# Another fill and drain for a group-normed dynamic 3x3 convolution block

## The chip, the cores and the metric

One core of a Trainium2 chip runs the kernel. The metric is the device time of one execution in microseconds (us). The engines are TensorE (PE), VectorE (DVE), ScalarE (ACT), GpSimd (POOL) and SyncE (SP); each takes its instructions in order and waits on semaphores that the others raise. SyncE issues every transfer of this kernel.

## The reference

The input x has 32 images of 256 channels and 48x48 pixels, in float32. What is computed:

```python
xn = gn(x)                                  # 32 groups of 8 channels, mean and variance of each
f = relu(Wc @ xn + bc)                      # 256 -> 64 channels
gk = relu(mean(xn) @ Wc.T + bc)             # 64 gains of an image
g_kern = gk[:, None] * Wkk + bkk            # 64 x 3 x 3
xm = xn.reshape(N, C, 3, 16, 3, 16).max((3, 5))     # maxima of 16 x 16 blocks
sk = relu(Wc @ xm + bc)                     # 64 x 3 x 3
dynW = relu(Wck[:, 0] * g_kern + Wck[:, 1] * sk + bck)    # the weights of a 64 -> 64 convolution of this image
y = conv3x3(f, dynW) + b_ad
out = x + Wf @ y + bf                       # 64 -> 256 channels
```

## The kernel before

Each channel pair of an image lies on one partition, so an image is two "halves" t of 128 partitions by 2304 pixels. x lies in a ring of RING = 7 images in SBUF, loaded AHEAD = 5 images in front, and the result is written over x in place.

For one image the steps are these. ScalarE takes the mean of each half (`channel_mean`, L482) and, with the group mean known, the sum of squares (`square_sum`, L470), each one pass over 2304 pixels. VectorE takes the block maxima (`outer_maxima` L684, `middle_maxima` L697). TensorE adds up the groups (`group_means` L976, `group_squares` L985, or both in one as `group_sums` L1000), VectorE makes the negated mean (L749) and the variance (L724), ScalarE its root (`deviation` L489), VectorE the scaled projection weights (`normalise`, up to L739). TensorE projects x to f (`project_f` L904), in three chunks, the last of them with the 11 feature columns that hold maxima and mean. ScalarE writes f twice from PSUM, rounded to f16 (f_hi, L517) and in f32 (L520), and GpSimd takes the remainder f_lo (`f_low` L406). From the features VectorE makes the gains (`gains` L660 to L665), GpSimd the convolution weights in four operations (`weight_sums` L394 to L399), ScalarE rounds them (`weights_high`, L528 and L529) and GpSimd takes their remainder (`weights_low` L415).

The convolution is the sum of three terms of f16 products, high by high, low weights by high f, high weights by low f (`conv_main` with term 0, 1, 2, L839), for 20 of 24 rows of each half of the image, and `conv_rest` (L879) for the remaining rows, which needs copies of f made by DMA (`stack_rows`). ScalarE moves the result to Y (`y_main_out` L456), VectorE that of the rest (L718). The output product runs in six units (`product` L914): four of 960 columns and two of 384. VectorE evicts a unit with bias and x added (L642); units in AIDED are evicted by ScalarE to `lone` (L441) and added to x by GpSimd (L371). SyncE stores a half image as soon as its units are in.

The order is written out by hand for each engine. In the loop of image i TensorE runs the terms of i, the projection of i + 1 and the units of i - 1. EARLY tells until which image the group sums come as separate means and squares. Ahead of the loop comes the fill: loads of x(0), then the constants, then more of x; `magnitudes`, `f_bounds` and `weight_bounds` on VectorE work out powers of two that keep f16 in range, and `scaled_weights` puts them into the weights; all of them are single small operations linked by waits. Behind the loop comes the drain: image 31 has its own list of units (LAST_UNITS), moves its accumulators with two engines (`y_main_last`), and is stored unit by unit (L315).

## Time and profile before

| | |
|---|---|
| median of 3 runs | 531.56 us (531.4 to 532.97) |
| the profiled execution | 531.4 us, span 529.6 us |
| busy share of PE, ACT, DVE, POOL | 93%, 86%, 74%, 65% |
| DMA | 157.91 MB, mean 298 GB/s |

The page cuts the span into 40 slices and gives the busy share of each in tenths. TensorE shows less than 9 in the first six slices (13 us each) and in the last one. An execution takes 1.8 us more than its span. Matmul ends are modelled, so a busy TensorE is not a TensorE at its peak; what counts is how its starts repeat.

### The profile page before, as it was taken

Reading aid. Unit: us, or ns where it says so; the run is one execution under the profiler, and the core shown is the slowest. Engines: PE = TensorE matmul, PEld = TensorE weight load, DVE = VectorE, ACT = ScalarE, POOL = GpSimd, SP = SyncE. Lnnn points to the kernel's source line nnn. Section 1 sums busy time; section 2 is a strip of 40 time slices with the busy share of each in tenths; the row PEclk is TensorE's granted clock in tenths of the full one; section 3 lists DMA queues with packets and bytes.
Section 4 is the critical chain, followed back from the end, with each engine's and each line's share of the span. In section 5 each row is a group of like instructions: output and inputs, shape, how many; then the busy total and the mean of one; then the engine's idle time right before and its main releaser. Section 6 shows DMA issues by size and latency. Waiting matters only on the chain.

```text
span 529.6 us, 17923 instructions
## 1 busy us (share of the span) xinstructions
PE 490.5 (93%) x7640; PEld 289.2 (55%) x7640; DVE 394.0 (74%) x635; ACT 456.4 (86%) x513; POOL 341.6 (65%) x231
## 2 busy tenths in 40 slices
PE   1577879999999999999999999999999999999993
PEld 1244536665555566655555566655555566555560
DVE  4653847878878877878788778878788778788463
ACT  4788979999999999999999999999999999997311
...
GB/s 333 418 188 193 143 230 264 307 312 308 324 349 361 335 314 293 341 324 328 316 360 355 317 292 345 301 329 336 334 356 347 325 318 300 212 190 193 194 222 320
DMA packets 48414, 157.91 MB, mean 298 GB/s; under 512 B 4688, under 2 KB 15440, under 8 KB 48336
## 3 DMA queue, kind: packets, MB, share of 16 engines
...
## 4 chain that ended last, share of the span: by engine, by line
PE 84%; DVE 1%; issue 1%; DVEq 0%
PE ps L839 32%; PE ps L914 23%; PE ps L904 22%; PE ps L879 7%; DVE X L642 1%; PE ps L1000 0%; DVEq L125 0%; DVE Y L711 0%
## 5 line engine op out<-in xcount | busy, mean ns | idle before, releaser
L642 DVE SCALAR_TENSOR_TENSOR X<-ps,out_bias,X 128x960 f32<-128x960 f32 (+1 forms) x161 | 156.3, 974 | 22.1 <-PE ps L914 22.0
L914 PE MATMUL ps<-Y,const 64*64 64x480 f32 (+1 forms) x1536 | 143.5, 489 | 0.8 <-DVE Y L711 0.8
L470 ACT ACTIVATE unused<-X,neg_mean 128x2304 bf16<-128x2304 f32 x64 | 140.8, 2201 | 1.8 <-DVE neg_mean L749 1.8
L482 ACT ACTIVATE unused<-X 128x2304 bf16<-128x2304 f32 x64 | 135.3, 2114 | 4.8 <-DMA X<-x 4.8
L904 PE MATMUL ps<-X,wcn_t 128*64 128x384 f32 (+1 forms) x768 | 134.0, 499 | 1.7 <-DVE wcn_t L739 1.7
L684 DVE TENSOR_REDUCE feats<-X 128x6 f32<-128x1536 f32 x64 | 109.3, 1744 | 6.7 <-DMA X<-x 6.7
L371 POOL TENSOR_TENSOR X<-X,lone 128x960 f32<-128x960 f32 x31 | 69.5, 2241 | 54.3 <-DVE wcn_t L739 45.0
L904 PEld LDWEIGHTS ps<-X,wcn_t 128*64 128x64 f32 x768 | 52.8, 138 | 74.1 <-issue 71.3
L394 POOL TENSOR_TENSOR dyn_a<-const,pool_g 128x576 f32<-128x576 f32 x32 | 37.0, 1156 | 73.9 <-DVE pool_g L665 73.9
L839 PE MATMUL ps<-f_hi,dyn_hi 64*64 64x480 f16 x1152 | 68.0, 371 | 5.9 <-issue 5.9
L914 PEld LDWEIGHTS ps<-Y,const 64*64 64x64 f32 x1536 | 61.6, 133 | 21.1 <-DVE Y L718 10.9
L415 POOL TENSOR_TENSOR dyn_lo<-dyn_b,dyn_hi 128x576 f16<-128x576 f32 x32 | 41.2, 1286 | 47.6 <-ACT dyn_hi L528 47.6
L406 POOL TENSOR_TENSOR f_lo<-f,f_hi 128x1152 f16<-128x1152 f32 x32 | 71.3, 2227 | 0.0
L839 PE MATMUL ps<-f_hi,dyn_lo 64*64 64x480 f16 x1152 | 69.7, 379 | 0.0
L839 PE MATMUL ps<-f_lo,dyn_hi 64*64 64x480 f16 x1152 | 66.8, 370 | 0.8 <-issue 0.8
L839 PEld LDWEIGHTS ps<-f_hi,dyn_hi 64*64 64x64 f16 x1152 | 49.5, 107 | 27.6 <-issue 19.4
L839 PEld LDWEIGHTS ps<-f_hi,dyn_lo 64*64 64x64 f16 x1152 | 48.5, 109 | 25.7 <-issue 15.0
L697 DVE TENSOR_REDUCE feats<-X 128x3 f32<-128x768 f32 x64 | 60.3, 942 | 0.0
L839 PEld LDWEIGHTS ps<-f_lo,dyn_hi 64*64 64x64 f16 x1152 | 32.5, 106 | 37.8 <-issue 18.6
L517 ACT ACTIVATE f_hi<-ps,f_bias 128x1152 f16<-128x1152 f32 x32 | 38.6, 1205 | 14.4 <-PE ps L904 14.4
L397 POOL TENSOR_TENSOR dyn_a<-dyn_a,dyn_b 128x576 f32<-128x576 f32 x32 | 45.2, 1412 | 2.5
L879 PE MATMUL ps<-stack,dyn_hi 64*64 64x192 f16 x1152 | 43.7, 244 | 0.6 <-DVE X L642 0.6
...
## 6 DMA issues: line engine op xcount, KB each, us to landing
...
```

The source lines that it names most:

```text
L371: nc.gpsimd.tensor_tensor(out, out, unit_lone(n), ALU.add).then_inc(added, 1)
L397: nc.gpsimd.tensor_tensor(dyn_a[:], dyn_a[:], dyn_b[:], ALU.add).then_inc(dyn_step, 1)
L406: nc.gpsimd.tensor_tensor(f_lo[inner], f32[:], f_hi[inner], ALU.subtract) \
L470: nc.scalar.activation(unused[:, t], pixels(u, t), ACT.Square, scale=1.0 / SIDE, bias=neg_mean[:, n % 2, 1:2], accum_out=feats[:, (n + 1) ...
L482: nc.scalar.activation(unused[:, t], pixels(u, t), ACT.Identity, scale=1.0 / PIX, accum_out=feats[:, n % 2, t, MEAN:MEAN + 1]).then_inc(me ...
L642: nc.vector.scalar_tensor_tensor(out=out, in0=unit_psum(piece, bank), scalar=out_bias[:, t:t + 1], in1=out, op0=ALU.add, op1=ALU.add).then ...
L684: nc.vector.tensor_reduce(feats[:, n % 2, t, 0:4 * K].rearrange("p (k l) -> p k l", k=2)[:, :, 0:K], X[:, at:at + 2 * pitch].rearrange("p ...
L697: nc.vector.tensor_reduce(feats[:, n % 2, t, K:2 * K], X[:, at:at + 2 * pitch].rearrange("p (k f) -> p k f", k=2)[:, :, 0:rows] .rearrange ...
L839: mm = nc.tensor.matmul(ps[CM * h:CM * (h + 1), CONV_BANKS[q], 0:MAIN], w[lanes, n % 2, tap, :], f[lanes, n % 2, r:r + MAIN_ROWS, LEFT - 1 ...
L879: mm = nc.tensor.matmul(ps[CM * h:CM * (h + 1), REST_BANK + q, 0:REST], w[lanes, n % 2, taps[h], :], f[lanes, n % 2, r:r + REST_ROWS, LEFT ...
L904: mm = nc.tensor.matmul(ps[CM * h:CM * (h + 1), F_BANK + c, 0:width], wcn_t[:, n % 2, t, :], X[:, at:at + width], start=(t == 0), stop=(t ...
L914: mm = nc.tensor.matmul(ps[rows, bank + q, col:col + width], wft[lanes, t, rows], Y[lanes, n % 2, at:at + width], start=True, stop=True)
```

## The change

- Constants come in two transfers, the first ahead of x(0), without the output weights and biases; x(0, 1) comes in two transfers.
- The bounds are worked out before the first statistics, and part of them, the scaling of the weights and three constant products (`per_gain`, `beside`) by GpSimd; the output bias and a copy to PSUM by ScalarE.
- For images 0 and 1 (SPLIT) the statistics of half 0 stay on ScalarE, now with the channel's own mean as shift; those of half 1 are made by VectorE with bn_stats on six strips of 384 pixels and one bn_aggr. The spread of the channel means within the group is added as a square of 2 columns.
- For these images (SUMS) VectorE makes the convolution weights in two pieces of taps (0 to 3, 4 to 8), from products that were prepared; ScalarE rounds each piece, and TensorE's first term waits for each. The features get products of their own behind the three chunks. In image 0 the term with f_lo comes before that with the low weights.
- EARLY is 3 and not 2; ScalarE's order in the fill is written out anew. Its pass for squares waits also for the means, and its eviction for the output bias. Image 1 has no unit aided.
- Images 29, 30 and 31 have other lists of units: none aided in 29, units 3 and 5 in 30, unit 2 in 31. The stores of image 29 go ahead of the stacking of f_lo of image 31. The last rest term goes to other banks (LAST_REST_BANK), all three terms of image 31 run before it, and ScalarE moves the last accumulators alone. Half of image 30 is stored by units too.

The core of the diff:

```diff
 ORDER = (1, 0, 2, 3, 4, 5)
-DIRECT = tuple(k for k in ORDER if k not in AIDED)
-LAST_UNITS = ((0, 2, 6), (1, 2, SHARED), (0, 0, 2), (0, 1, 6), (1, 0, 0), (1, 1, SHARED))
-LAST_AIDED = 2
-EARLY = 2
-UNAIDED = 1
+PENULT_UNITS = ((0, 0, 6), (0, 1, 2), (0, 2, SHARED), (1, 0, 6), (1, 2, 2), (1, 1, 6))
+PENULT_AIDED = (3, 5)
+LAST_UNITS = ((0, 2, 2), (1, 2, SHARED), (0, 0, 0), (0, 1, 2), (1, 0, 6), (1, 1, SHARED))
+LAST_AIDED = (2,)
+EARLY = 3
+SPLIT = (0, 1)
+STRIPS = 6
+STRIP = PIX // STRIPS
...
+        def aided(n):
+            if n < UNAIDED or n == N - 3:
+                return ()
+            return {N - 2: PENULT_AIDED, N - 1: LAST_AIDED}.get(n, AIDED)
+        def direct(n):
+            order = ORDER if n < N - 2 else range(UNITS)
+            return tuple(k for k in order if k not in aided(n))
...
+            late = first["wf_t"]
+            sp.dma_start(const[:, 0:late], consts[:, 0:late]).then_inc(const_in, 16)
             load(0, 0)
-            load(0, 1)
-            sp.dma_start(const[:], consts).then_inc(const_in, 16)
+            second = xd[0, :, 1, :].rearrange("p (s f) -> p s f", s=2)
+            for s, sem_in in enumerate((first_rows, loaded[0][1])):
+                sp.dma_start(pixels(0, 1)[:, s, :], second[:, s, :]).then_inc(sem_in, 16)
+            sp.dma_start(const[:, late:], consts[:, late:]).then_inc(late_in, 16)
             for n in range(1, AHEAD):
                 load(n, 0)
                 load(n, 1)
...
                 if i + AHEAD < N:
                     load(i + AHEAD, 0)
                     load(i + AHEAD, 1)
-                stack_rows(f_lo, 1, i + 1)
-                if i > 0:
+                if i == N - 2:
                     store(i - 1, 0)
                     store(i - 1, 1)
-            for k in (0, 1, 3, 2, 4, 5):
-                store_last(k)
+                stack_rows(f_lo, 1, i + 1)
+                if 0 < i < N - 2:
+                    store(i - 1, 0)
+                    store(i - 1, 1)
+            store(N - 2, 0)
+            store_unit(N - 2, 4)
+            store_unit(N - 2, 3)
+            store_unit(N - 1, 0)
+            store_unit(N - 1, 1)
+            store_unit(N - 2, 5)
+            for k in (3, 2, 4, 5):
+                store_unit(N - 1, k)
             for b in range(RING):
                 for t in range(HALVES):
...
+                nc.gpsimd.tensor_tensor(per_gain, w0, by_gain, ALU.mult).then_inc(early_const, 1)
+                nc.gpsimd.tensor_tensor(beside, w0, by_one, ALU.mult).then_inc(scale_step, 1)
+                pool.wait_ge(scale_step, 3)
+                nc.gpsimd.tensor_tensor(beside, beside, b0, ALU.add).then_inc(early_const, 1)
+                pool.wait_ge(bias_mm, 1)
+                nc.gpsimd.tensor_scalar(wft[:], wft[:], bnd[:, 5:6], bnd[:, 13:14], ALU.mult, ALU.mult) \
...
             def leave(n, k, t, piece, bank):
                 wait(act, added, evacuations(n, k) - 2)
                 act.wait_ge(out_mm, count(n, k + 1, UNITS))
-                nc.scalar.activation(unit_lone(n), unit_psum(piece, bank), ACT.Identity,
+                act.wait_ge(bias_known, HALVES)
+                nc.scalar.activation(unit_lone(n, k), unit_psum(piece, bank), ACT.Identity,
                                      bias=out_bias[:, t:t + 1]).then_inc(evacuated, 1)
...
-            def square_sum(t, n):
+            def square_sum(t, n, ahead=0):
                 u, lap = n % RING, n // RING
                 if inside(n):
                     act.wait_ge(neg_ready, count(n, 1))
-                    wait(act, squares, n, t - 1, HALVES)
+                    act.wait_ge(squares, halves_done(n - 1, t))
+                    act.wait_ge(means, halves_done(n + ahead, t))
...
+            def own_mean(n):
+                k = splits(n) - 1
+                wait_loaded(act, n, 0, 0)
+                if n > 0:
+                    act.wait_ge(means, halves_done(n - 1, 0))
+                nc.scalar.activation(unused[:, 0], pixels(n, 0), ACT.Identity, scale=1.0 / PIX,
+                                     accum_out=own[:, k, 0, 0:1]).then_inc(means, 1)
+                act.wait_ge(means, halves_done(n, 0))
+                nc.scalar.activation(shift[:, k:k + 1], own[:, k, 0, 0:1], ACT.Identity,
+                                     scale=-1.0 / SIDE).then_inc(shifted, 1)
+            def own_squares(n):
+                k = splits(n) - 1
+                act.wait_ge(shifted, splits(n))
+                if n > 0:
+                    act.wait_ge(squares, halves_done(n - 1, 1))
+                nc.scalar.activation(unused[:, 1], pixels(n, 0), ACT.Square, scale=1.0 / SIDE,
+                                     bias=shift[:, k:k + 1], accum_out=own[:, k, 0, 1:2]).then_inc(squares, 1)
...
+            def spread_square(n):
+                act.wait_ge(neg_ready, n + 1)
+                nc.scalar.activation(feats[:, (n + 1) % 2, :, SQ], own[:, splits(n) - 1, :, 0], ACT.Square,
+                                     bias=neg_mean[:, n % 2, 0:1]).then_inc(spread_ready, 1)
...
+            copy_kk()
+            own_mean(0)
+            own_squares(0)
+            output_bias()
+            spread_square(0)
+            keep_mean(0)
             deviation(0)
+            own_mean(1)
+            own_squares(1)
             features(0)
-            channel_mean(0, 1)
-            channel_mean(1, 1)
-            f_out(0)
-            weights_high(0)
-            square_sum(0, 1)
-            square_sum(1, 1)
+            f_high(0)
+            early_high(0, 0)
+            f_full(0)
+            early_high(0, 1)
+            early_relu(0)
+            channel_mean(0, 2)
+            spread_square(1)
+            keep_mean(1)
             deviation(1)
+            channel_mean(1, 2)
+            y_main_out(0)
+            square_sum(0, 2)
             features(1)
-            channel_mean(0, 2)
-            y_main_out(0)
-            channel_mean(1, 2)
-            f_out(1)
-            weights_high(1)
-            for i in range(1, EARLY):
-                square_sum(0, i + 1)
-                square_sum(1, i + 1)
-                deviation(i + 1)
-                features(i + 1)
-                channel_mean(0, i + 2)
-                channel_mean(1, i + 2)
-                f_out(i + 1)
-                y_main_out(i)
-                weights_high(i + 1)
-                unit(3, i - 1)
-            square_sum(0, EARLY + 1)
-            square_sum(1, EARLY + 1)
-            channel_mean(0, EARLY + 2)
-            channel_mean(1, EARLY + 2)
+            f_high(1)
+            early_high(1, 0)
+            f_full(1)
+            early_high(1, 1)
+            early_relu(1)
+            square_sum(1, 2)
+            channel_mean(0, 3)
+            deviation(2)
+            features(2)
+            channel_mean(1, 3)
+            channel_mean(0, 4, 2)
+            f_out(2)
+            square_sum(0, 3, 1)
+            y_main_out(1)
+            weights_high(2)
+            square_sum(1, 3)
+            channel_mean(1, 4)
+            deviation(3)
+            features(3)
+            channel_mean(0, 5, 2)
+            channel_mean(1, 5, 2)
+            f_out(3)
+            y_main_out(2)
+            weights_high(3)
+            square_sum(0, 4, 1)
+            square_sum(1, 4, 1)
             for i in range(EARLY, N):
                 deviation(i + 1)
                 features(i + 1)
...
+            def early_sums(n, piece):
+                if piece == 0:
...
+                shape = [P, PIECE_AT[piece + 1] - PIECE_AT[piece], CM]
+                w1 = ck[:, 1:2, :].to_broadcast(shape)
+                s = mean_act[:, n % 2, taps].unsqueeze(2).to_broadcast(shape)
+                a, b = dyn_a[:, taps, :], dyn_b[:, taps, :]
+                nc.vector.tensor_tensor(b, w1, s, ALU.mult).then_inc(early_step, 1)
+                nc.vector.scalar_tensor_tensor(out=a, in0=per_gain[:, taps, :],
+                                               scalar=mean_act[:, n % 2, MEAN:MEAN + 1],
+                                               in1=beside[:, taps, :], op0=ALU.mult, op1=ALU.add) \
+                    .then_inc(early_step, 1)
+                dve.wait_ge(early_step, done + 2)
+                nc.vector.tensor_tensor(a, a, b, ALU.add).then_inc(early_step, 1)
...
+            def strip_stats(n, s):
+                if n == 0 and s == 0:
+                    dve.wait_ge(first_rows, 16)
+                else:
+                    wait_loaded(dve, n, 0, 1)
+                for k in range(STRIPS // 2):
+                    nc.vector.bn_stats(strips[:, STRIPS // 2 * s + k, :],
+                                       pixels(n, 1)[:, s, STRIP * k:STRIP * (k + 1)]).then_inc(strip_ready, 1)
+                if s == 1:
+                    dve.wait_ge(strip_ready, STRIPS * splits(n))
+                    nc.vector.bn_aggr(own[:, splits(n) - 1, 1, :], strips[:]).then_inc(own_ready, 1)
...
-            maximum(1, 0)
             magnitudes()
+            f_bounds()
+            strip_stats(0, 0)
+            strip_stats(0, 1)
+            middle_maxima(0, 0)
             negate_mean(0)
-            f_bounds()
-            weight_bounds()
+            weight_scale()
+            middle_maxima(1, 0)
             variance(0)
             normalise(0)
-            scaled_weights()
+            outer_maxima(0, 0)
+            outer_maxima(1, 0)
+            strip_stats(1, 0)
             gains(0)
-            maximum(0, 1)
+            for piece in range(PIECES_OF_SUMS):
+                early_sums(0, piece)
+            strip_stats(1, 1)
+            middle_maxima(0, 1)
             negate_mean(1)
-            maximum(1, 1)
-            maximum(0, 2)
+            middle_maxima(1, 1)
             variance(1)
             normalise(1)
+            outer_maxima(0, 1)
+            negate_mean(2)
+            outer_maxima(1, 1)
+            middle_maxima(0, 2)
             gains(1)
-            maximum(1, 2)
-            negate_mean(2)
+            for piece in range(PIECES_OF_SUMS):
+                early_sums(1, piece)
             y_rest_out(0)
+            outer_maxima(0, 2)
+            outer_maxima(1, 2)
             for i in range(1, N - 1):
-                if i > 1:
-                    middle_maxima(1, i + 1)
+                middle_maxima(1, i + 1)
                 variance(i + 1)
...
                 unit(3, i - 1)
                 unit(4, i - 1)
                 unit(5, i - 1)
-            unit(1, N - 2)
-            unit(0, N - 2)
+            for k in range(UNITS):
+                unit(k, N - 2)
             y_rest_out(N - 1)
-            unit(2, N - 2)
-            unit(4, N - 2)
-            unit(5, N - 2)
-            unit_last(0)
-            unit_last(1)
-            y_main_last()
-            for k in (3, 4, 5):
-                unit_last(k)
+            for k in range(UNITS):
+                unit(k, N - 1)
...
                     dy, dx = divmod(tap, K)
+                    if term == 0 and n < SUMS and tap in PIECE_AT[1:]:
+                        pe.wait_ge(dyn_hi_ready, highs_done(n, PIECE_AT.index(tap)))
...
+            def project_early(n, between):
+                begin_f(n)
+                project_chunk(n, 0)
+                between()
+                for c in range(1, CHUNKS):
+                    project_chunk(n, c)
...
             setup()
+            group_means(0)
             group_squares(0)
-            project_f(0)
+            project_early(0, lambda: None)
+            project_features(0)
+            conv_main(0, 0)
             group_means(1)
-            conv_main(0, 0)
+            conv_main(2, 0)
+            group_squares(1)
             conv_main(1, 0)
-            group_squares(1)
-            conv_main(2, 0)
-            project_f(1)
-            group_means(2)
+            project_early(1, lambda: group_means(2))
+            project_features(1)
...
             conv_main(0, N - 1)
-            unit(0, N - 2)
-            unit(1, N - 2)
+            unit_penult(0)
+            unit_penult(1)
             conv_main(1, N - 1)
+            unit_penult(2)
+            unit_penult(3)
+            conv_main(2, N - 1)
+            unit_penult(4)
             conv_rest(N - 1)
-            unit(2, N - 2)
-            unit(3, N - 2)
-            unit(4, N - 2)
-            unit(5, N - 2)
-            unit_last(0)
-            unit_last(1)
-            conv_main(2, N - 1)
-            for k in range(2, UNITS):
+            unit_penult(5)
+            for k in range(UNITS):
                 unit_last(k)
```

## Rows read from the trace of the kernel before

**Rows 1.** The page: chain that ended last, shares of the span.
```profile
PE 84%; DVE 1%; issue 1%; DVEq 0%
```

**Rows 2.** Windows: PE, PEld, DVE, ACT, POOL busy; PE clock, DMA share, GB/s.
```profile
30.00:35.00 5.00, 5.00 (x74) 2.41 (x69) 1.46 (x2) 4.35 (x4) 2.08 (x2) 0.66 0.56 203
60.00:75.00 15.00, 9.98 (x116) 5.35 (x108) 7.80 (x14) 14.22 (x17) 3.47 (x2) 0.77 0.87 323
300.00:450.00 150.00, 150.00 (x2384) 88.74 (x2384) 121.06 (x191) 142.21 (x163) 106.22 (x71) 1.00 0.88 328
526.00:528.00 2.00, 0.00 (x0) 0.00 (x0) 0.00 (x0) 0.00 (x0) 0.00 (x0) 0.50 0.76 305
```

**Rows 3.** Timeline of TensorE in the drain: start us, us, then the instruction.
```profile
488.90 2.10 PE L839 MATMUL ps<-f_hi,dyn_hi 64*64 64x480 f16 x36
...
503.88 2.10 PE L839 MATMUL ps<-f_hi,dyn_hi 64*64 64x480 f16 x36
...
517.07 0.60 PE L839 MATMUL ps<-f_lo,dyn_hi 64*64 64x480 f16 x6 [0.77 <-issue]
518.42 3.45 PE L914 MATMUL ps<-Y,const 64*64 64x480 f32 x32 [0.76 <-DVE Y L711]
```

**Rows 4.** Timeline of ScalarE in the middle.
```profile
262.37 0.68 ACT L528 ACTIVATE dyn_hi<-dyn_a 128x576 f16<-128x576 f32 x1
262.94 0.68 ACT L529 ACTIVATE dyn_b<-dyn_a 128x576 f32<-128x576 f32 x1
263.52 1.05 ACT L441 ACTIVATE lone<-ps,out_bias 128x960 f32<-128x960 f32 x1
...
266.47 0.20 ACT L482 ACTIVATION_READ_ACCUMULATOR unused<-X 128x1 f32 x1
267.45 0.20 ACT L489 ACTIVATE norm<-norm 128x1 f32<-128x1 f32 x1 [0.78 <-DVE norm L724]
```

**Rows 5.** Timeline of VectorE: the variance of image 4.
```profile
87.47 0.22 DVE L724 TENSOR_SCALAR norm<-ps 128x1 f32<-128x1 f32 x1 [0.66 <-PE ps L1000]
```

**Rows 6.** The page: costliest groups, busy us, mean ns of one, idle before.
```profile
L470 ACT ACTIVATE unused<-X,neg_mean 128x2304 bf16<-128x2304 f32 x64 | 140.8, 2201 | 1.8 <-DVE neg_mean L749 1.8
L482 ACT ACTIVATE unused<-X 128x2304 bf16<-128x2304 f32 x64 | 135.3, 2114 | 4.8 <-DMA X<-x 4.8
L684 DVE TENSOR_REDUCE feats<-X 128x6 f32<-128x1536 f32 x64 | 109.3, 1744 | 6.7 <-DMA X<-x 6.7
...
L394 POOL TENSOR_TENSOR dyn_a<-const,pool_g 128x576 f32<-128x576 f32 x32 | 37.0, 1156 | 73.9 <-DVE pool_g L665 73.9
...
L406 POOL TENSOR_TENSOR f_lo<-f,f_hi 128x1152 f16<-128x1152 f32 x32 | 71.3, 2227 | 0.0
...
L517 ACT ACTIVATE f_hi<-ps,f_bias 128x1152 f16<-128x1152 f32 x32 | 38.6, 1205 | 14.4 <-PE ps L904 14.4
```

**Rows 7.** Timeline of all engines in the first 33 us.
```profile
6.41 2.12 ACT L482 ACTIVATE unused<-X 128x2304 bf16<-128x2304 f32 x1 [4.18 <-DMA X<-x]
...
10.31 1.01 PE L810 MATMUL ps<-const 64*128 64x1 f32 x4 [10.31 <-DMA const<-consts]
...
18.32 0.22 DVE L724 TENSOR_SCALAR norm<-ps 128x1 f32<-128x1 f32 x1 [1.64 <-PE ps L985]
...
19.91 6.02 PE L904 MATMUL ps<-X,wcn_t 128*64 128x395 f32 x24 [1.71 <-DVE wcn_t L739]
...
29.47 2.81 PE L839 MATMUL ps<-f_hi,dyn_hi 64*64 64x480 f16 x36 [3.33 <-issue]
...
32.13 2.95 PE L839 MATMUL ps<-f_hi,dyn_lo 64*64 64x480 f16 x36
```

**Rows 8.** Timeline of VectorE and of SyncE's queue in the drain.
```profile
520.33 3.47 DVE L642 SCALAR_TENSOR_TENSOR X<-ps,out_bias,X 128x960 f32<-128x960 f32 x3 [1.97 <-PE ps L914]
...
508.20 8.42 SPq L304 DMA_DIRECT2D out<-X  x4
516.66 7.91 SPq L315 DMA_DIRECT2D out<-X  x6
```

418 lines of the change are left out of this document (265 added, 153 removed).

## The prediction, made before the changed kernel was run

> **What bounds the kernel now.** I read the chain of waits first: TensorE carries 84% of it, and what is left lies at the two ends [rows 1]. The windows say where. From 300 to 450 us TensorE is busy for all of 150.00 us, at granted clock 1.00 (the upper level, 2.4 GHz); between 60 and 75 us it works 9.98 of 15 and the clock is 0.77 [rows 2]. So the middle can't get shorter by this change: it is one image per 14.98 us (first term of image 30 at 488.90, of image 31 at 503.88 [rows 3]). What can move is the time until this rhythm starts and the time after it. 32 times 14.98 is 479.4 of 529.6; fill and drain are the other 50.
>
> Two facts of the middle matter for the change. ScalarE has no slack to speak of: from the standard deviation of one image (L489) to its last mean it works back to back, 14.20 us, then waits 0.78 for the sums that TensorE makes of these means (266.47+0.20 to 267.45) [rows 4]; 14.20+0.78 is again 14.98. In the fill the same engine is the one that ends last: it must have done the squares of image 3 and the means of image 4 before TensorE can go on, and that is where TensorE loses the time between 60 and 75 us. And a met wait costs ScalarE nothing: L528 to L529 (no wait between) is 0.57 us start to start, L529 to L441 (two waits) 0.58 [rows 4].
>
> I measure the phase of the rhythm at one event, the variance of image 4 (L724), which in the kernel before starts at 87.47 [rows 5]; everything after it repeats by 14.98.
>
> **The fill, step by step.** Prices: a ScalarE pass over half an image 2.11 (mean) and 2.20 (square), f_hi 1.2, f_lo on GpSimd 2.23, its product of 576 columns 1.16, VectorE's maximum over 1536 columns 1.74 [rows 6] (the one over 768 half of it). These are durations; on ScalarE the next starts some 0.1 before the end, so I count 2.11, 2.20 and 1.11 from start to start.
>
> - Loads. Between 6.41 (first half image landed) and 10.31 (constants landed) 1.18+0.44 MB came in, 415 GB/s [rows 7]. With 0.31 MB of constants ahead: constants at about 4.3, x(0,0) at 7.15, the two quarters of x(0,1) at 8.6 and 10.0, the late constants at 10.3. The first ScalarE pass starts 0.7 later than before, which costs nothing, as VectorE's half ends last.
> - Setup. The eight linked operations of the bounds (1.9 us in all) run from 5.9 to 7.8, before any image is there; they stood between mean and variance. The four steps that go to GpSimd have no price here: a 1-column operation lies between nothing and the 1.16 of 576 columns, so 0 to 4.6 us from 7, done by 12 and needed at 12.8. Its three scalings and three products of 576 columns are done between 17 and 21 and needed at 23.2. Both at nothing, hidden by the maxima and the projection.
> - First statistics. bn_stats isn't in the trace. By the rate of the maximum (1.74 us for 1536 columns, so 0.44 for 384) three of them take 1.4; twice that is my upper end, since it makes two results. I take the low value, because it reads the same columns once, like the maximum. Half 1: 10.0+1.4+0.3 (aggregate) = 11.7. Mean of the group known at 12.1, negated at 12.8 behind one maximum. ScalarE's own squares end at 12.0; what remains is one 0.2 us square of a mean, so the group variance starts on VectorE at 14.3 behind the second maximum, against 18.32. From variance to projection 19.91-18.32 = 1.6, so the projection starts at 15.9 and not 19.91 [rows 7]: 4.0 won.
> - First weights. The projection takes 6.0 as before, its 4 feature products (0.7) now last, and features are ready on VectorE at 22.8. Before, four GpSimd operations of 1.16 and more and a ScalarE pass lay between the features and the first term at 29.47 [rows 7]. Now VectorE makes piece 0 in three operations of 256 columns (1.35 with the gaps: L642 takes 1.16 for 960 columns [rows 8], which is 0.31 for 256, and I add 0.14 to each), ScalarE rounds it (0.3), f_hi in between: first term at 25.15. 4.3 won. Piece 1 is ready at 26.5; the term waits some 0.4 for it.
> - The f_lo term now goes before the low weights: f_lo at 28.6 (ScalarE's f32 to 26.2, GpSimd 2.2). Both terms end at 32.7, and the projection of image 1 begins there.
> - Images 1 to 3. From 23.2 on ScalarE is nearly full: its work up to the squares of image 4 is 3 f_out of 2.2, 2 split ones with pieces (3.4 each), 9 means and 7 squares of the full kind, and the small ones, 47.5 us; it idles 1.6 for the variance of image 1, 1.1 for the features of image 1, 1.1 each for the projections of 2 and 3, and 1.5 in small gaps, 6.3 in all. 23.2+47.5+6.3 = 77.0. TensorE reaches the same place at 76.5 (first terms of images 1, 2 and 3 at 40.0, 58.0 and 73.8; each follows from the rounded weights on ScalarE, and the projection before it from a deviation there plus 1.5). L724 of image 4: 77.0+0.5 = 77.5, against 87.47: 10.0 won. Two full passes of both sorts per image less on ScalarE for two images (8.6 us) less about 1.5 of small ones make most of this; the earlier start the rest.
> - From this I take 1.0 for the clock. Before, TensorE idled 3.3 us ahead of the first term and ran it in 2.81 and the next term in 2.95 instead of 2.10 [rows 3, 7], with a granted clock of 0.66 from 30 to 35 us [rows 2]. This is 1.6 us. After the change it idles 2.3 + 0.4 + 0.7 in about the same place, so the drop is likely; part of it falls into the wait for piece 1. Fill: 9.0 won.
>
> A rule that speaks here: the Trainium skill (TensorE: Matmul & The Clock Gate, Part 1) says that the array gets the lower clock after idling and the upper one only after sustained work. By it every short idle of the new fill is a risk, and the sum would be the clock rival's below; the row from 30 to 35 us agrees with the fall.
>
> - Added waits in the loop: two per image on the squares' passes and one on the eviction, ScalarE only. Nothing by [rows 4]; behind them are the rest of ScalarE's queue and TensorE's next sums (see the slow rival).
>
> **The drain.** Before, the first term of image 31 starts at 503.88; its last term broke off for 0.77 "issue" [rows 3], and only then came the eviction of the accumulators and the last four units at 518.42; VectorE's last three evictions ran from 520.33 to 523.80, SyncE's last store was out at 524.57, and the span ended 5.0 later [rows 3, 8]. The DMA engines were also loaded: the stores of image 29 went out at 508.20 only, behind the stacking of f_lo, and the share is still 0.76 from 526 to 528 [rows 2, 8].
>
> After: image 29 has all its units on VectorE (one more, 1.2, hidden in VectorE's idle), and its stores go ahead of the f_lo stacking, at 503.0 and 506.1. That moves 2.36 MB out of the end; the stacking queues behind the second (landed by 511, needed at 512.9). TensorE from 504.1: three terms of 1.9 to 2.0 with four units between them to 512.9 (a unit is 0.82 or 0.33), rest term to 514.2, then unit 5 of image 30 and the six last ones to 519.0, against 521.9. VectorE is then the one behind: y_rest to 514.8, two evictions of 0.6 to 516.6, then 1.2 each from 517.3 to 520.8. GpSimd adds (30,5) to 518.4 and (31,2) to 520.7. SyncE waits for that one, then sends three stores at 520.7, 521.1 and 521.6; their 1.5 MB need 3.6 us. Last issue out at 522.1 against 524.57, last byte at 525.2 against about 527.5: 2.3 won. If the 0.77 break comes back, 1.5.
>
> **Sum.** The profiled run took 531.4 with a span of 529.6 (the median is 531.56). 531.4 - 9.0 - 2.3 = 520.1.
>
> **The rivals.**
> 1. The clock stays low through more of the fill. The kernel before also had a granted clock of 0.77 from 60 to 75 us [rows 2]. If the short idles do this again in image 1 or 2, one more term of 2.10 nearly doubles (1.8); with the whole of the 1.6 above, 1.6-1.0+1.8 = 2.4 are lost: 522.5. For: the fill keeps six gaps of 0.4 to 2.3. Against: the stall of over 4 us before the 0.77 goes away. By the skill's rule named above it would be this.
> 2. The end is bound by bytes and by GpSimd: 5 of the last 6 large units are only ready in the last 3 us, and the stores queue as before. Drain at nothing: 522.4. For: the DMA share of 0.76 as late as 526 to 528 [rows 2]. Against: image 29 is out of the way.
> 3. VectorE is late in the fill: bn_stats at twice its price (1.4 at image 0, 0.5 at image 1 beyond its slack), aggregate and pieces with two SBUF inputs at 1.5 times (1.4). Sum 3.3: 523.4.
> 4. Slower. ScalarE's loop of 14.20+0.78 is as long as TensorE's, so whatever a met wait costs there is paid in each of 28 images. Three waits more; with 0.1 us of slack the turning point is (11.3/28+0.1)/3 = 0.17 us per wait; at 0.25, somewhat over its smallest operation (0.20), it is 0.65 x 28 = 18: 538. Against: 0.57 and 0.58 in [rows 4].
> 5. The change does not do what it says, ScalarE's total in the fill being kept by the waits on VectorE and TensorE: only the first 4.0 us and the drain come, 525.1.
>
> **Chances.** Forecast 0.52, clock 0.16, drain 0.12, VectorE late 0.10, no more than the start 0.06, slower 0.04. Range 517.8 to 524.5: below, no clock loss (1.0) and gaps that I counted twice (1.3); above, the first three rivals with 1 us for two coming together. Faster by over 0.3% (what can be told from no change here): 0.95; within 0.01; slower 0.04.
>
> **What would show it.** L904 of image 0 starts at 15.9 (start step), the first L839-type term at 25.15 (weights), L724 of image 4 at 77.5, TensorE's busy share 10 tenths from there, period 14.98; a granted clock under 1.00 only around 28 to 33 us. In the drain the stacking of f_lo lands before the rest term, and SyncE's last store is out near 522.1-9.0 = 513.1. Wrong would be: a period over 14.98, a fill whose ScalarE idles more than 6.3 us between 23 and 77, or bn_stats over 0.6 us.

## The result, and the profile after

The changed kernel takes 519.34 us (median, 518.51 to 520.02) against 531.55 of the kernel before beside it: a ratio of 0.977, 95% interval 0.976 to 0.979. The forecast was 520.1. The profiled run took 519.18 with a span of 517.5; the sums below are made against this span and the 529.6 of before.

The first view is the page of the changed kernel: its span, its busy times, two rows of its slices (12.9 us each) and the chain's shares.

```profile
span 517.5 us, 18003 instructions
...
PE 488.6 (94%) x7668; PEld 285.5 (55%) x7668; DVE 402.8 (78%) x649; ACT 451.1 (87%) x515; POOL 343.7 (66%) x233
...
PE   1698999999999999999999999999999999999993
...
PEclk9999999999999999999999999999999999999998
...
PE 83%; ACT 1%; DVE 0%; DVEq 0%; issue 0%; ACTq 0%
```

TensorE is at 6 tenths in the second slice already and full from the fifth on. It still carries the chain, as in [rows 1]: what bounds the middle has not changed.

Where the 12.1 us of span went shows in one event that both traces have, the variance step on VectorE (L926 now). This is VectorE's timeline at images 0, 4 and 31 (start us, us, instruction, and what ended the idle before it):

```profile
13.67 0.21 DVE L926 TENSOR_SCALAR norm<-ps 128x1 f32<-128x1 f32 x1
...
77.60 0.22 DVE L926 TENSOR_SCALAR norm<-ps 128x1 f32<-128x1 f32 x1 [1.53 <-PE ps L1266]
...
482.38 0.22 DVE L926 TENSOR_SCALAR norm<-ps 128x1 f32<-128x1 f32 x1 [0.66 <-PE ps L1266]
```

Before, image 4 stood at 87.47 [rows 5] and image 31 at 491.93, by the same timeline of the kernel before:

```profile
491.93 0.22 DVE L724 TENSOR_SCALAR norm<-ps 128x1 f32<-128x1 f32 x1 [0.66 <-PE ps L1000]
```

So three numbers carry the result: the fill is 87.47 - 77.60 = 9.87 shorter; the middle, 27 images, takes 404.78 instead of 404.46, 0.32 longer; the drain, from image 31's variance to the end of the span, takes 35.12 instead of 37.67, 2.55 shorter. 9.87 - 0.32 + 2.55 = 12.1.

The windows of the changed kernel that answer to [rows 2], and two from its drain (busy us of PE, PEld, DVE, ACT, POOL; PE clock, DMA share, GB/s):

```profile
30.00:35.00 5.00, 5.00 (x70) 3.13 (x64) 3.59 (x8) 3.67 (x5) 0.00 (x0) 1.00 0.51 179
60.00:75.00 15.00, 14.45 (x238) 9.49 (x234) 11.95 (x19) 13.67 (x18) 8.77 (x7) 1.00 0.78 289
...
506.00:510.00 4.00, 3.50 (x40) 1.16 (x32) 3.18 (x4) 1.79 (x2) 3.13 (x2) 1.00 0.51 179
510.00:516.00 6.00, 0.00 (x0) 0.00 (x0) 1.43 (x2) 0.00 (x0) 1.28 (x1) 0.70 1.01 406
```

In this trace the two dips of the clock are gone, 0.66 and 0.77 before, 1.00 now (three kernels with the same waits still show the first one, see experiment 7), and TensorE works 14.45 of the 15 us in which it had worked 9.98. In the drain the DMA engines are still full, but for the last 6 us only.

### The profile page after: what moved, and what is told of

Same layout as the page of the kernel before. It is cut to its first block, busy times and chain, and to the rows that moved or that the text cites. A ratio compares the mean times of both kernels' runs of the same rounds, so it can differ in the third digit from the quotient of the medians.

```text
span 517.5 us, 18003 instructions
## 1 busy us (share of the span) xinstructions
PE 488.6 (94%) x7668; PEld 285.5 (55%) x7668; DVE 402.8 (78%) x649; ACT 451.1 (87%) x515; POOL 343.7 (66%) x233
## 4 chain that ended last, share of the span: by engine, by line
PE 83%; ACT 1%; DVE 0%; DVEq 0%; issue 0%; ACTq 0%
PE ps L1053 32%; PE ps L1154 22%; PE ps L1119 22%; PE ps L1093 7%; ACT unused L575 1%; PE ps L1266 1%; DVE X L815 0%; DVEq L135 0%; ACT dyn_b L687 0%; ACT dyn_hi L686 0%; ACTq L574 0%
## 5 line engine op out<-in xcount | busy, mean ns | idle before, releaser
L575 ACT ACTIVATE unused<-X,neg_mean 128x2304 bf16<-128x2304 f32 x60 | 132.1, 2202 | 0.4 <-DVE neg_mean L952 0.4
L588 ACT ACTIVATE unused<-X 128x2304 bf16<-128x2304 f32 x60 | 126.6, 2111 | 0.2
L483 POOL TENSOR_TENSOR X<-X,lone 128x960 f32<-128x960 f32 x30 | 67.2, 2240 | 48.6 <-DVE wcn_t L941 41.3
L1053 PE MATMUL ps<-f_hi,dyn_lo 64*64 64x480 f16 x1152 | 66.9, 368 | 0.1
L503 POOL TENSOR_TENSOR dyn_a<-const,pool_g 128x576 f32<-128x576 f32 x30 | 34.9, 1164 | 44.2 <-DVE pool_g L839 44.2
L1053 PEld LDWEIGHTS ps<-f_hi,dyn_hi 64*64 64x64 f16 x1152 | 48.4, 106 | 27.5 <-issue 13.9
L1053 PEld LDWEIGHTS ps<-f_hi,dyn_lo 64*64 64x64 f16 x1152 | 45.4, 106 | 24.9 <-issue 13.4
L1053 PEld LDWEIGHTS ps<-f_lo,dyn_hi 64*64 64x64 f16 x1152 | 32.7, 106 | 36.8 <-issue 17.2
L508 POOL TENSOR_TENSOR dyn_a<-dyn_a,const 128x576 f32<-128x576 f32 x30 | 42.7, 1423 | 2.4
L506 POOL TENSOR_TENSOR dyn_a<-dyn_a,dyn_b 128x576 f32<-128x576 f32 x30 | 42.4, 1413 | 2.4
```

The source lines that it names most:

```text
L483: nc.gpsimd.tensor_tensor(out, out, unit_lone(n, k), ALU.add).then_inc(added, 1)
L506: nc.gpsimd.tensor_tensor(dyn_a[:], dyn_a[:], dyn_b[:], ALU.add).then_inc(dyn_step, 1)
L508: nc.gpsimd.tensor_tensor(dyn_a[:], dyn_a[:], b0, ALU.add).then_inc(dyn_step, 1)
L575: nc.scalar.activation(unused[:, t], pixels(u, t), ACT.Square, scale=1.0 / SIDE, bias=neg_mean[:, n % 2, 1:2], accum_out=feats[:, (n + 1) ...
L588: nc.scalar.activation(unused[:, t], pixels(u, t), ACT.Identity, scale=1.0 / PIX, accum_out=feats[:, n % 2, t, MEAN:MEAN + 1]).then_inc(me ...
L1053: mm = nc.tensor.matmul(ps[CM * h:CM * (h + 1), CONV_BANKS[q], 0:MAIN], w[lanes, n % 2, tap, :], f[lanes, n % 2, r:r + MAIN_ROWS, LEFT - 1 ...
```

## The experiments

Each edit is made in the changed kernel, and each kernel was timed beside the kernel before (531.12 to 531.19 us). "V0", "V1", "V4" and "V31" stand for the start of the variance step of images 0, 1, 4 and 31, and "tail" for V31 to the end of the span. In the changed kernel: V1 30.67, V4 77.60, V31 482.38, tail 35.12, 519.34 us. The start of the program wanders by some tenths: V0, ahead of nearly all edits, lies between 13.45 and 14.29 (13.67 in the changed kernel). What wanders most is the projection of image 0: it took 5.51 to 6.78 us over the fourteen kernels, 6.53 in the changed one, and whatever follows moves with it. The stretch from its end with the feature products (22.69 in the changed kernel) to V4 does not: 54.91 in the changed kernel, and 54.87 to 54.94 in all kernels without an edit behind it but that of experiment 12. So effects in the fill are read from this stretch where they lie behind the projection. V4 alone went from 77.40 to 77.94 in kernels whose fill was not edited, and the medians of kernels whose edit shows in no V went down to 518.43: no effect is read from a difference under 0.5 us in V4, or under 1 us in a median alone.

**1. GpSimd's products of image 0 later.** In the changed kernel the weights of the normalised 1x1 convolution of image 0 (wcn_t, L941), one small VectorE step on the path to the first projection, took 1.07 us. Timeline of all engines:

```profile
14.68 1.16 POOL L472 TENSOR_TENSOR X<-const 128x576 f32<-128x576 f32 x1
14.85 1.07 DVE L941 TENSOR_SCALAR wcn_t<-const,norm 128x128 f32<-128x128 f32 x1
...
31.86 0.35 DVE L941 TENSOR_SCALAR wcn_t<-const,norm 128x128 f32<-128x128 f32 x1
```

The same step takes 0.35 for image 1, where GpSimd idles. The edit, on GpSimd ahead of the products:

```diff
+                pool.wait_ge(wcn_ready, 1)
                 w0, b0 = (ck[:, k:k + 1, :].to_broadcast([P, TAPS, CM]) for k in (0, 2))
```

> The changed kernel with one wait more: GpSimd starts its three constant products only when VectorE has written the projection weights of image 0. In the trace of the changed kernel that VectorE step (L941) took 1.07 us beside a running GpSimd product, and 0.35 in every other image. Theory of the shared access: L941 back to 0.35, projection of image 0 at 15.25 and not 15.97, and as the fill is one chain from there, the variance of image 4 (L926) at about 76.9 and not 77.60, total 518.6. Rival, the step is long for another reason (first use of the weights): L941 stays at 1.07 and the products come too late or no later, total 519.3 to 519.9. Rival, the chain is set by ScalarE's total: L941 0.35, but L926 of image 4 within 0.2 of 77.60, total 519.3.

Measured: 518.21 us (518.02 to 518.78). The same stretch of this kernel:

```profile
14.96 0.35 DVE L942 TENSOR_SCALAR wcn_t<-const,norm 128x128 f32<-128x128 f32 x1
...
15.36 2.19 PE L1120 MATMUL ps<-X,wcn_t 128*64 128x384 f32 x6 [1.75 <-DVE wcn_t L942]
15.39 1.16 POOL L473 TENSOR_TENSOR X<-const 128x576 f32<-128x576 f32 x1 [0.56 <-DVE wcn_t L942]
```

The step is back at 0.35, the projection starts at 15.36 instead of 15.97, and V4 is at 77.14, 0.46 earlier. So GpSimd's product held VectorE up by 0.72. From variance to projection it is 0.72 less (1.58 for 2.30); the projection took 6.69 here instead of 6.53, and from its end to V4 the two kernels agree (54.90 and 54.91). V4 alone would not show a gain of this size above its scatter. The kernels that kept the order show the same pair, 1.06 to 1.08 beside a product issued 0.16 to 0.18 earlier. The Trainium skill (SBUF — State Buffer, "Who interferes with whom") says that such a scaling on VectorE can take the memory ports that it shares with GpSimd, and that whichever issues second waits for the other's whole instruction. The trace agrees nearly: VectorE ended 0.08 after the product's end, where a full wait and then 0.35 of work would make it 0.35.

**2. An even column under GpSimd's last sum.** The sum that adds b0 (L508, L399 before) takes 1.42 us an image now and took 1.21 before.

```diff
     "kk": 2 * TAPS,
+    "even": 1,
     "ck": 3 * CM,
```

> The changed kernel with one unused column of constants ahead of the combination weights, so that they begin at an even float column again, as in the kernel before (406; after the change 147). Theory: GpSimd's addition of the bias (L508) takes 1.42 us and not 1.21 because of the odd column; with the pad it goes back to 1.21, ScalarE no longer waits for it in the middle, no period of 15.02 is left, and the variance of image 31 comes 0.3 to 0.4 earlier (482.38 before the pad), total 519.0. Rival: the step is longer because of what runs beside it; L508 stays at 1.42 and the total at 519.3.

Measured: 518.59 us, the sum still 1.42, V31 482.23. An odd starting column is not it; experiment 12 takes this up again.

**3. Twelve more met waits an image on ScalarE.**

```diff
                     act.wait_ge(means, halves_done(n + ahead, t))
+                    for _ in range(3):
+                        act.wait_ge(pads_zero, 1)
```

and the same ahead of the squares' passes.

> The changed kernel with three more waits, on a semaphore long at its value, ahead of each of ScalarE's four passes of an image, 12 more per image from image 2 on. The forecast's step: a met wait costs ScalarE nothing, so the period stays at 14.98 and the total at 519.3. The slow rival (0.17 us per wait or more): 12 x 0.17 x 28 = 57 us, total over 576. In between, 0.02 us per wait would be 12 x 0.02 x 28 = 6.7, total 526.

Measured: 518.43 us, V4 77.49, V31 482.27: 404.78 for 27 images, as in the changed kernel, though made up otherwise (no image of 15.02 or 15.03, but 15.15 for the last; why was not looked at). TensorE's group sums start 0.10 to 0.12 behind ScalarE's last mean, as against 0.12, and never late against TensorE's own rhythm. So twelve met waits cost ScalarE some 0.02 us an image at most, and the prediction's slow rival, which needed 0.17 for one, has no price left.

**4. One more small operation on ScalarE per image.**

```diff
                 channel_mean(1, i + 3)
+                if inside(i + 3):
+                    nc.scalar.activation(more[:, 1:2], spare[:, 0:1], ACT.Identity)
```

> The changed kernel with one operation of one column more on ScalarE in each of 26 images (some 0.11 us from start to start), right ahead of the group sums it has to be in time for. If ScalarE's loop (14.20 of work and 0.78 of waiting) is as long as TensorE's, the period grows to 15.09 and the total by 26 x 0.11 = 2.9, to 522.2. If ScalarE has slack, as TensorE's 100% busy share says, nothing: 519.3.

Measured: 518.97 us; V4 77.85, V31 482.34. ScalarE's timeline of this kernel at image 17:

```profile
271.90 0.19 ACT L589 ACTIVATION_READ_ACCUMULATOR unused<-X 128x1 f32 x1
271.99 0.19 ACT L764 ACTIVATE more<-spare 128x1 f32<-128x1 f32 x1
272.82 0.20 ACT L641 ACTIVATE norm<-norm 128x1 f32<-128x1 f32 x1 [0.64 <-DVE norm L929]
```

In the changed kernel the wait ahead of that step is 0.73 at this image. The operation went into the wait, and the 27 images took 404.49. But this does not test ScalarE's slack: the operation stands behind the last mean, and TensorE's sums wait for the mean, not for it, so it would have cost nothing under either expectation.

The traces that are there answer the question. This is the changed kernel, first ScalarE's last mean and TensorE around the sums (L1266) in an ordinary image, then the same one image later:

```profile
196.78 0.19 ACT L588 ACTIVATION_READ_ACCUMULATOR unused<-X 128x1 f32 x1
196.29 1.03 PE L1154 MATMUL ps<-Y,const 64*64 64x480 f32 x8
197.10 0.29 PE L1266 MATMUL ps<-feats,const 64*64 64x4 f32 x4
...
211.86 0.19 ACT L588 ACTIVATION_READ_ACCUMULATOR unused<-X 128x1 f32 x1
211.27 1.03 PE L1154 MATMUL ps<-Y,const 64*64 64x480 f32 x8
212.15 0.28 PE L1266 MATMUL ps<-feats,const 64*64 64x4 f32 x4
```

In the ordinary image the sums start 0.81 behind the unit's first product and 0.13 behind the end of the mean (0.12 in most images). In the other one the mean came 0.10 later against the rhythm, and the sums start 0.88 behind the product and 0.10 behind the mean: TensorE waited for ScalarE. With 0.10 as the least distance, ScalarE has 0.02 us to spare in an ordinary image. In the kernel before, the distance was 0.17, so it had 0.07.

**5. The new fill with the old drain.** The lists and the order of units, the place of the last rest term, the two engines that move the last accumulators, and the order of the stores, all as in the kernel before, behind the new fill. Its core:

```diff
-PENULT_AIDED = (3, 5)
+PENULT_AIDED = (3,)
...
-            if n < UNAIDED or n == N - 3:
+            if n < UNAIDED:
...
-                if i == N - 2:
-                    store(i - 1, 0)
-                    store(i - 1, 1)
                 stack_rows(f_lo, 1, i + 1)
-                if 0 < i < N - 2:
+                if 0 < i < N - 1:
```

> The changed kernel with the drain of the kernel before: its lists of units, its order, its moves of the last accumulators, whole stores of images 29 and 30, the stores of 29 behind the stacking. One part alone. By the two traces, the stretch from the variance of image 31 to the end is 37.67 us before (491.93 to 529.6) and 35.12 after (482.38 to 517.5), so this kernel should have the fill of the change (variance of image 4 at 77.6) and the tail of before (37.7), total 2.5 above the changed kernel: 521 to 522. Rival: the drain's gain comes only because the fill has moved the loads and stores; then the tail is 35 to 36 here also, total 519.

Measured: 522.03 us (521.75 to 522.3), V31 482.83, tail 37.87 against the 37.67 of the kernel before. So the two parts add up, and the drain's is worth 37.87 - 35.12 = 2.75.

**6. Image 1's statistics on ScalarE alone**, by full passes, as before the change:

```diff
-SPLIT = (0, 1)
+SPLIT = (0,)
...
-            own_mean(1)
-            own_squares(1)
+            channel_mean(0, 1)
+            channel_mean(1, 1)
```

with the matching moves of the squares, and without VectorE's strips of image 1.

> The changed kernel with the statistics of image 1 whole on ScalarE (mean and shifted squares of both halves), as in the kernel before; image 0 stays split. ScalarE gets one mean pass and one square pass more (2.11+2.20), and both square passes of image 1 now wait for its group mean. Theory, the fill is bound by ScalarE: its two squares run from 28.4 to 32.8, the variance of image 1 moves from 30.67 to about 33.3, and of image 4 from 77.60 to about 81 (3 to 4.3 more), total 522 to 523. Rival, VectorE and the chain through TensorE bind the fill and ScalarE's idle time (3.5 us before f_hi of image 0 alone) takes the passes: variance of image 4 under 78.6, total 520 at most.

Measured: 522.32 us. V1 33.07 (2.40 later), V4 81.59 (3.99 later), V31 486.21. ScalarE's timeline of this kernel:

```profile
28.19 2.22 ACT L575 ACTIVATE unused<-X,neg_mean 128x2304 bf16<-128x2304 f32 x1 [1.08 <-DVE neg_mean L952]
...
30.40 2.20 ACT L575 ACTIVATE unused<-X,neg_mean 128x2304 bf16<-128x2304 f32 x1
```

What this adds to ScalarE's queue, four passes for two and the small steps of the split, comes out at V4 as 3.99 (3.79 from the end of the first projection). In this part of the fill ScalarE is the bound.

**7. The first weights in one piece.**

```diff
-PIECE_AT = (0, 4, TAPS)
+PIECE_AT = (0, TAPS)
```

> The changed kernel with the first weights of images 0 and 1 in one piece (PIECE_AT = (0, 9)), not in taps 0 to 3 and 4 to 8. Two things are told apart. The pieces' own worth: the first term of image 0 starts at 25.95 and not at 24.96 but runs through, f_hi's f32 copy and f_lo come about 1.05 later (28.33 to 29.4), likewise about 0.6 for image 1; variance of image 4 at 78.3 to 79.0, total 520 to 520.7. And the clock: TensorE idles 3.2 us ahead of the first term here, as the 3.33 in the kernel before. Clock rival: the term takes 2.8 us and not 2.1, the granted clock between 28 and 34 us falls under 1.00, and the variance of image 4 comes 1 to 1.6 later than by the pieces alone (79.5 to 80.5).

Measured: 521.09 us, V1 31.51, V4 79.35 (1.75 later). TensorE's timeline and two windows of this kernel:

```profile
25.47 3.22 PE L1051 MATMUL ps<-f_hi,dyn_hi 64*64 64x480 f16 x36 [3.54 <-issue]
...
28.84 2.40 PE L1051 MATMUL ps<-f_lo,dyn_hi 64*64 64x480 f16 x36
```

```profile
26.00:28.00 2.00, 2.00 (x28) 1.15 (x23) 1.18 (x3) 2.00 (x3) 1.43 (x1) 0.54 1.03 422
28.00:30.00 2.00, 1.95 (x28) 1.15 (x24) 1.08 (x2) 1.48 (x4) 2.00 (x2) 0.61 1.05 421
```

Behind an idle of 3.54 the granted clock was at 0.54, near the lower level (1.2 GHz), and the first two terms took 3.22 and 2.40 instead of 2.10 and 2.07: 1.45 more. The first projection happened to take only 5.70 here. Counted from its end, the first term starts 1.27 later than with two pieces (3.54 for 2.27) and V4 comes 2.50 later; 1.45 of that is the slow terms, and about 1.05 the missing piece, as expected.

That the longer idle brought the clock down is not shown by this, for three other kernels have the idles of the changed one (2.27, then 0.39) and their clock fell too: those of experiments 4 and 11, and that of 12. A window and a term of experiment 4, then of 12:

```profile
26.00:28.00 2.00, 2.00 (x25) 0.97 (x21) 1.97 (x6) 2.00 (x4) 1.72 (x1) 0.50 1.03 417
25.19 3.51 PE L1056 MATMUL ps<-f_hi,dyn_hi 64*64 64x480 f16 x36 [2.27 <-ACT f_hi L668]
...
26.00:28.00 2.00, 2.00 (x29) 1.03 (x21) 1.85 (x5) 2.00 (x2) 2.00 (x2) 0.50 1.01 407
27.59 2.91 PE L1053 MATMUL ps<-f_lo,dyn_hi 64*64 64x480 f16 x36
```

In 4 and 11 the clock fell early. The whole loss went into the first term, and this ran through the two waits (for piece 1 and for f_lo) that TensorE has there anyway: V4 is at 54.93 and 54.94 from the projection's end, no later. In 12 it fell later, the f_lo term took 2.91, and V4 came at 55.50, 0.6 later. The other seven kernels with these idles kept 1.00. What decides between them is open.

**8. The new fill in another order.** The same instructions, moved: on ScalarE the means and squares of image 2 come earlier, on VectorE the last strips of image 1 and the maxima of image 2, on TensorE the group sums of images 1 and 2, and the wait of experiment 1 is in. Its core on ScalarE:

```diff
+            channel_mean(0, 2)
             features(0)
...
-            channel_mean(0, 2)
...
-            deviation(1)
...
+            deviation(1)
...
+            square_sum(1, 2)
```

> The changed kernel with another order in the fill and no other work: ScalarE takes the first mean of image 2 in the 3.5 us it idles ahead of f_hi of image 0 and the second mean and second square of image 2 earlier; VectorE makes the last three strips of image 1 in its idle 2.1 us ahead of the gains and the outer maxima of image 2 ahead of the gains of image 1; TensorE sums the groups of images 1 and 2 as soon as they are there; GpSimd's constant products wait as in the run before. Theory, ScalarE's work and its forced idles set the fill: 3 to 4 us of passes leave the stretch behind 37 us, the variance of image 4 comes at 74.5 to 75.5 and not at 77.6, total 516.5 to 517.5. Rival, a chain through TensorE (projection, f, weights, terms of image after image) sets it: variance of image 4 not before 76.9, total 518.3.

Measured: 517.06 us (516.76 to 517.41), ratio to the kernel before 0.973, interval 0.971 to 0.975: the fastest kernel of this study. V1 27.89 (2.78 earlier), V4 75.83 (1.77 earlier), tail 35.08. The total lies in the expected range; V4 was expected at 74.5 to 75.5 and gained 1.8, somewhat less. The first projection ends at 22.69 as in the changed kernel (V0 is 0.55 late, and the wait of experiment 1 makes up for it), so that the 1.77 is what the order alone is worth. A loss is visible: ScalarE, now ahead, idles for TensorE instead, as its timeline shows:

```profile
49.70 1.22 ACT L668 ACTIVATE f_hi<-ps,f_bias 128x1152 f16<-128x1152 f32 x1 [1.79 <-PE ps L1123]
```

In the changed kernel this wait is 0.95. Once ScalarE is freed the bound alternates with TensorE, which the expectation left out.

**9. Image 0's last two terms swapped on TensorE.**

```diff
-            conv_main(2, 0)
-            group_squares(1)
             conv_main(1, 0)
+            group_squares(1)
+            conv_main(2, 0)
```

> Only image 0's order on TensorE is turned round: the low weights' term before the f_lo term, as in the kernel before; GpSimd still makes f_lo first and the low weights after it, ready at 29.52. Theory (the new order is worth what GpSimd needs for the low weights): the low weights' term starts at 29.6 instead of the f_lo term at 28.33, both end 1.3 later, the projection of image 1 starts at 33.75 instead of 32.46, ScalarE waits 2.2 instead of 0.90 for the features of image 1, variance of image 4 at 78.9 and 520.6 us. Rival (ScalarE's own queue hides it, its gaps being shorter than the delay elsewhere): variance of image 4 within 0.4 of 77.60 and 519.3 to 519.7.

Measured: 521.03 us, V4 79.72 (2.12 later, though V0 was 0.22 earlier). TensorE's timeline and two windows:

```profile
28.86 2.83 PE L1053 MATMUL ps<-f_hi,dyn_lo 64*64 64x480 f16 x36 [1.64 <-POOL dyn_lo L527]
...
31.86 2.80 PE L1053 MATMUL ps<-f_lo,dyn_hi 64*64 64x480 f16 x34
```

```profile
30.00:32.00 2.00, 2.00 (x32) 1.20 (x28) 0.00 (x0) 0.00 (x0) 0.00 (x0) 0.50 1.00 385
32.00:34.00 2.00, 2.00 (x31) 1.77 (x29) 1.52 (x6) 1.64 (x2) 0.00 (x0) 0.66 0.24 64
```

The wait for the low weights came as expected, and nothing hid it. What was not expected is the price on top: behind a wait of only 1.64, the third in this stretch after 2.27 and 0.39, the clock fell to 0.50, and the two terms took 0.7 each more. From the end of the first projection (21.98 here) V4 comes 2.83 later: the expected 1.3 and the 1.4 to 1.5 of the slow terms. The new order of the terms saves the first; that it also saves the second is a matter of where the clock falls (experiment 7).

**10. Image 29's unit 3 added by GpSimd.**

```diff
-            if n < UNAIDED or n == N - 3:
+            if n < UNAIDED:
```

> Only unit 3 of image 29 changes: GpSimd adds it again, as it does for every image in the middle, instead of VectorE. Theory (the second store of image 29 waits for GpSimd, and the stacking of f_lo of image 31 queues behind it on SyncE, so that the rest term of image 31 comes late): variance of image 31 unchanged at 482.4, time from there to the end of the span 36.3 instead of 35.12, 520.5 us. Rival (the stacking has room enough, and what ends the kernel is VectorE's last three evictions whatever comes before): 35.1 and 519.3 us.

Measured: 520.63 us (520.22 to 521.42), V31 482.32, tail 36.68 (1.56 later). SyncE's queue (start, us of issuing) and TensorE's rest term in this kernel:

```profile
493.39 6.62 SPq L369 DMA_DIRECT2D out<-X  x2
500.05 0.48 SPq L390 DMA_DIRECT2D stack<-f_lo  x1
```

```profile
504.58 0.24 PE L1093 MATMUL ps<-stack,dyn_hi 64*64 64x192 f16 x1 [1.40 <-DMA stack<-f_lo]
```

The stores of image 29 held the queue for 6.62 instead of 3.21, the stacking went out at 500.05 instead of 497.44, and TensorE waited 1.40 for it. The edit that looks like a trifle, one add moved to VectorE, is a condition for the stores to stand ahead of the stacking at all.

**11. Image 29's stores behind the stacking.**

```diff
-                if i == N - 2:
-                    store(i - 1, 0)
-                    store(i - 1, 1)
                 stack_rows(f_lo, 1, i + 1)
-                if 0 < i < N - 2:
+                if 0 < i < N - 1:
```

> Only the order on SyncE changes: the two stores of image 29 go out behind the stacking of f_lo of image 31, not ahead of it. Theory of the prediction (2.36 MB moved out of the end is what the drain gains, as the DMA engines are full in the last 7 us): from the variance of image 31 to the end of the span 36.4 instead of 35.12, 520.6 us. Rival (the engines still have room from 500 to 508, where the stores now fall, so the bytes are done before the last ones queue): 35.1 to 35.4 and 519.3 to 519.6 us.

Measured: 521.98 us (521.92 to 522.72), V31 482.69, tail 38.41, 3.3 longer, more than either theory said. Windows of this kernel, then the same three of the changed kernel:

```profile
492.00:500.00 8.00, 8.00 (x149) 5.64 (x143) 6.29 (x7) 1.99 (x3) 4.30 (x3) 1.00 0.08 18
500.00:508.00 8.00, 8.00 (x164) 5.42 (x158) 2.99 (x6) 3.90 (x4) 3.37 (x2) 1.00 0.98 387
508.00:518.00 10.00, 1.49 (x16) 0.31 (x8) 3.42 (x3) 0.25 (x1) 3.29 (x2) 0.74 1.03 396
```

```profile
492.00:500.00 8.00, 8.00 (x142) 5.62 (x134) 6.29 (x7) 1.68 (x3) 4.00 (x3) 1.00 0.72 281
500.00:508.00 8.00, 7.88 (x158) 4.97 (x152) 2.97 (x6) 3.89 (x4) 3.35 (x2) 1.00 0.76 283
508.00:518.00 10.00, 1.50 (x16) 0.30 (x8) 3.43 (x3) 0.27 (x1) 3.28 (x2) 0.72 0.69 273
```

TensorE, VectorE, ScalarE and GpSimd do the same in both, and VectorE's last three evictions start at 507.95 and 507.96. What differs is the DMA engines: idle from 492 to 500 (0.08 instead of 0.72), then full to the end. The 2.36 MB are 5.8 us of work at 405 GB/s, and 3.3 of them come out at the end. Without this one move the rest of the drain's changes gains nothing: that kernel ends later than the one with the old drain (38.41 against 37.87). Whether the move alone would gain as much was not tried.

**12. b0 at its old address.** Three columns of the constants move ahead of the array that holds w0, w1 and b0, so that it starts at column 150, not 147; all else stays in place. In bytes, b0 then lies where it lay before the change, but for exactly 1024.

```diff
     "kk": 2 * TAPS,
+    "b_ad": 1,
+    "bf": HALVES,
     "ck": 3 * CM,
```

> Only three columns of the constants move (the bounds' and the biases' ones go ahead of the array that holds w0, w1 and b0), so that this array starts at byte 24 of a 64-byte line, as in the kernel before, and not at byte 12; all other buffers keep their addresses. Theory (GpSimd's last sum of an image takes 1.42 us instead of 1.21 because of where b0 lies): back to 1.21, and the slips of 0.01 to 0.04 per image in the middle go away, so that image 31 is reached 27 times 14.98 after image 4, 0.3 earlier; 519.0 us. Rival (it depends on something else, such as the place of the summed buffer): 1.42 stays and 519.3 us.

Measured: 518.62 us (518.55 to 519.64). GpSimd's groups between 150 and 450 us, of this kernel and of the changed one:

```profile
L508 POOL TENSOR_TENSOR dyn_a<-dyn_a,const 128x576 f32<-128x576 f32 x20 | 24.1, 1205 | 1.6
```

```profile
L508 POOL TENSOR_TENSOR dyn_a<-dyn_a,const 128x576 f32<-128x576 f32 x20 | 28.4, 1422 | 1.6
```

The address it is: 1.21 again. (Experiment 2 had moved b0 and the buffer behind it together, so it could not tell a column from a distance.) Whether b0's own address or its distance to the summed buffer counts stays open. It does touch ScalarE, whose rounding of the weights waits for this sum: TensorE's group sums now start 0.17 behind ScalarE's last mean, as before the change, and not 0.12, so the slower sum had taken 0.05 of ScalarE's 0.07 us of slack. But it is not what slips in the middle: the 27 images took 404.68, and single images of 15.02 and 15.03 are still there.

## Why the prediction was right, step by step

**Start.** Forecast: projection of image 0 at 15.9; measured 15.97. Errors cancelled. Everything up to the variance was early: it was forecast at 14.3 and came at 13.67, as the first half image landed at 6.79 and not 7.15, and VectorE's bn_stats, 0.49 a piece (2.86 for six), ran close to the price that I took from the maximum. Then GpSimd's three products, "at nothing, hidden", cost 0.72 on VectorE (experiment 1). This is the step that failed: hidden from the path is not hidden from a neighbour that is on the path. The prediction asked only when the products were due. In the next step two more errors cancelled: the projection took 6.53 and not 6.0, and its feature products, counted as 0.7 on top, added only 0.2.

**First weights.** Forecast: first term at 25.15, f_lo term at 28.6, both ended at 32.7. Measured (TensorE's timeline of the changed kernel):

```profile
24.96 1.03 PE L1053 MATMUL ps<-f_hi,dyn_hi 64*64 64x480 f16 x16 [2.27 <-ACT f_hi L667]
26.38 1.23 PE L1053 MATMUL ps<-f_hi,dyn_hi 64*64 64x480 f16 x20 [0.39 <-ACT dyn_hi L693]
...
28.33 2.07 PE L1053 MATMUL ps<-f_lo,dyn_hi 64*64 64x480 f16 x36 [0.41 <-POOL f_lo L518]
```

All within 0.3, idles of 2.3, 0.4 and (0.41, not 0.7) included.

**Clock.** Here 1.0 was taken off, and nothing was lost: the granted clock is 1.00 throughout the fill of this trace. The rival that the prediction put on the Trainium skill's rule (TensorE: Matmul & The Clock Gate, Part 1) did not come either. That is in part luck. Of the ten kernels with these idles (2.27, 0.39) three lost the clock behind these idles, and V4 lost 0, 0 and 0.6 by it, as the slow first term ran through the waits (experiment 7). So the mechanism was right, and so was the remark that part of the loss falls into the wait for piece 1; the size of 1.0 was too large for every one of the ten. With one piece, or with the terms swapped (7 and 9), there are no such waits to hide in, and it cost about 1.4.

**Images 1 to 3.** First terms forecast at 40.0, 58.0 and 73.8; measured 39.75, 57.53 and 73.18. V4 was 77.5 and came at 77.60. So the total of the ledger of ScalarE's work held: between 23 and 77 it was busy for 48.47 (forecast 47.5) and idle for 5.53 (forecast 6.3). Its items did not. Those named (3 f_out, 2 split ones, 9 means, 7 squares) already add up to 47.8 without the small ones; the trace has 2, 2, 8 and 6 of them there, and three moves to Y and the rounding of the weights of images 2 and 3, which the ledger does not name. One too many of each of three kinds (6.5) made up for these. Experiment 6 shows that ScalarE's load is what decides.

**The middle.** The period was to stay 14.98; it mostly does, but seven images took 15.02 to 15.03, which with the 15.00 of the first makes the 0.32, within the rounding. Six of the seven stand in pairs, and in each pair TensorE's group sums started 0.42 instead of 0.34 behind the matmul before them, and 0.10 behind ScalarE's last mean (at 212.15, 302.14 and 452.06): ScalarE was late and TensorE waited for it, as the lines in experiment 4 show. Met waits (experiment 3) and the slower sum (12) do not make ScalarE late in these images; what does was not found. "ScalarE has no slack to speak of" was right: 0.07 us before, 0.02 now. The slow rival rested on this and on a price per wait; only the price is gone.

**Drain.** Forecast 2.3, measured 2.55 (2.75 by experiment 5). Last store out forecast at 513.1; SyncE's queue of the changed kernel:

```profile
493.55 3.21 SPq L369 DMA_DIRECT2D out<-X  x2
497.44 0.47 SPq L390 DMA_DIRECT2D stack<-f_lo  x1
...
503.95 9.11 SPq L377 DMA_DIRECT2D out<-X  x9
```

503.95 + 9.11 = 513.06, the stacking was out by 500, and the break of 0.77 in the last term [rows 3] did not return. But the ranking of causes was off: the prediction led with TensorE's and VectorE's last units, and named the bytes second. Experiment 11 has the same units at the same times and is 3.3 slower. The rival "the end is bound by bytes" was right on the mechanism; it did not come because image 29's bytes were out of the way, as the prediction held against it.

**Sum.** 10.0 forecast for the fill before the clock, 9.87 measured; 1.0 for the clock, 0; drain 2.3, 2.55; middle 0, -0.32. Forecast 11.3 of span, measured 12.1.
